# Local attention on TensorE: mask and both halves of a tile's scores issued in one go

## The chip, the cores and the metric

The kernel runs on one core of one Trainium2 chip. The metric is the device time of that core in microseconds (us); less is better. Of the engines the text uses the profile's short names: PE is TensorE (matrix products and transposes), DVE is VectorE, ACT is ScalarE, POOL is GpSimd, SP issues DMAs.

## What is computed

The reference has two residual layers; the part that takes most of the time, and the only one that the change touches, is a stack of six local-attention layers on 8 sequences of 512 tokens with 128 features, 16 heads of 64, windows of 32:

```python
for i in range(DEPTH):            # DEPTH = 6
    x = attn_layer(shift_tokens(x), Wqkv[i], q_scale[i], k_scale[i], Wo[i]) + x
    x = ffn_layer(shift_tokens(x), ln_g[i], ln_b[i], W1[i], b1[i], W2[i], b2[i]) + x

# attn_layer, per head: q and k normalised and rotated; each window of 32 queries sees
# its own 32 keys and the 32 before them
mask = (it < jb) | (it > jb + w) | (jb == -1)
sim = jnp.einsum('bhwie,bhwje->bhwij', bq, bk2) * QK_SCALE
sim = jnp.where(mask, -jnp.finfo(sim.dtype).max, sim)
attn = jax.nn.softmax(sim, -1)
out = jnp.einsum('bhwij,bhwje->bhwie', attn, bv2)

# ffn_layer
a, gate = jnp.split(hg, 2, -1)
return a * jax.nn.gelu(gate, approximate=False) @ W2 + b2
```

All of it is in float32, the mask excepted, which is added as a bf16 product.

## The kernel before

The kernel has three passes. The first (up to about 1190 us) does the global attention, the experts and the chunked attention; the last one adds and writes out. Between them stands `transformer`, the local-attention pass. It runs a hardware loop over the six layers, and in each trip of it the eight sequences are written out, so there are 48 passes through one list of steps, which the text calls trips. A trip mixes two sequences: it begins the attention of one while the rest of the one before (tile 3's scores and outputs, the feed-forward part) still has to be done.

The order of the steps within a trip is the list `BODY`, written by hand (L190 to L199), and every engine walks through it, doing its own share of each step. A sequence is four tiles of 128 tokens, and the first number of a step is its tile `t`: `qk.t.j` and `v.t.j` are projections (one product, 128 rows by 512 columns), `t.t.j` turns a quarter of the queries (j = 0, 1) or keys (2, 3), `sa.t` and `s.t.p` are the scores of a tile for the two parities p of heads, `n` and `w` are work of DVE and ACT alone (norms; sums of the softmax), `pt.t.k` turns half of the probabilities, `oa.t` and `o.t.p` multiply them by the values, `y` is the output projection, `xt`, `xn`, `gate.c`, `up.c` and `y2` are the feed-forward part. Nothing on PE leaves this order: the engine works through it one instruction after the other, and waits where a semaphore isn't there yet.

The list of a trip is:

```python
BODY = [step(name) for name in """
    qk.0.0 t.3.0 qk.0.1 t.3.1 t.3.2 qk.0.2 t.3.3 qk.0.3 n.0 pt.2.0 qk.1.0 sa.3
    v.0.0 pt.2.1 s.3.0 s.3.1 v.0.1 t.0.0 t.0.1 w.3 t.0.2 qk.1.1 t.0.3 oa.2
    qk.1.2 o.2.0 o.2.1 qk.1.3 pt.3.0 sa.0 n.1 pt.3.1 v.1.0 s.0.0 s.0.1 qk.2.0
    v.1.1 t.1.0 w.0 t.1.1 oa.3 t.1.2 qk.2.1 o.3.0 o.3.1 t.1.3 qk.2.2 pt.0.0
    qk.2.3 v.2.0 sa.1 pt.0.1 qk.3.0 s.1.0 s.1.1 n.2 w.1 y v.2.1 t.2.0
    t.2.1 xt oa.0 t.2.2 t.2.3 o.0.0 o.0.1 qk.3.1 pt.1.0 pt.1.1 xn qk.3.2
    qk.3.3 sa.2 v.3.0 gate.0 s.2.0 s.2.1 gate.1 up.0 gate.2 v.3.1 w.2 oa.1
    up.1 up.2 n.3 o.1.0 o.1.1 y2
""".split()]
```

What PE does for a tile's scores is in `fill` (L1445). At `sa.t` it takes the two banks of PSUM (waiting for their last readers) and waits for the copies of the turned queries and keys, writes the mask into both (8 products in bf16, L1458) and does the first half of the products, `score_half` with pairs 0 to 3 (L1424). At `s.t.0` it does the second half (pairs 4 to 7); at `s.t.1` it does nothing. A product there uses 64 rows of the array and makes 32 by 64 results; 32 products make a half, which show as 64 records, since a float32 product is carried out twice. Two such steps per tile, four tiles per trip.

The eight banks of PSUM go round in a ring: the step that fills a bank waits until the reader of the step eight slots before is through. `sa` and `oa` have no slot of their own; they take those of `s` and `o`.

After a tile's scores DVE takes the row maxima and subtracts them (`negmaxl`, `probl`), ACT takes the exponential, DVE sums, POOL multiplies by the reciprocals (L1394), and PE turns the result (`pt`, L1502). After a projection of queries or keys DVE multiplies by the rotation tables (`cs`, L1691), ACT squares, DVE sums, ACT makes the reciprocal norms (L1558, L1559), and POOL adds the rotated halves (L1368) and multiplies by the norms (`qk`, L1377), four operations per tile; PE then turns the result (`t`, L1497). In the feed-forward part ACT computes the gelu (`gel`, L1605), DVE the gated product (`hf`, L1722), and PE the last product `y2` (L1528), which DVE adds to the state; the next trip's first rotations stand behind that on DVE.

The tail after the 48 trips (`OF_LAST`, L200) does what the last sequence has left; in it `sa.3` stands directly before `s.3.0`.

Of the kernel before, what the change touches and what calls it, by code (L numbers as in the profile page):

```python
# [40 lines left out]
PAIRSL = INNER // P  # L41
# [48 lines left out]
def settle(eng, passed):  # L90

    eng.sem_inc(passed, 1)  # L92
# [65 lines left out]
PARITIES = 2  # L158
# [1015 lines left out]
def transformer(nc, io, sh, buf, ctx, order):  # L1174

    last_part = order is OF_LAST
    ident, identb, maskw, state, psum = sh.ident, sh.identb, sh.maskw, sh.state, sh.psum
# [9 lines left out]
    def sem(name):  # L1187
        return ctx.enter_context(nc.semaphore(name + ("_tail" if last_part else "")))
# [46 lines left out]
    def readers(key):  # L1235
        kind, at = key[0], key[1:]
        if kind == "qk":
            return [(squared, at)]
        if kind == "v":
            return [(vcopied, at)]  # L1240
        if kind == "t":
            return [(tcopied, at)]
        if kind == "s":
            return [(centered, at)]
        if kind == "pt":
            return [(turned, at)]
        if kind == "o":
            return [(ocopied, at)]
        if kind == "y":
            return [(mid, "xm")]  # L1250
        if kind == "xt":
            return [(ffn, "x2")]
        if kind == "xn":
            return [(affine, "x2T")]
        if kind == "gate":
            return [(gelued, at[0])]
        if kind == "up":
            return [(hidden, at[0])]
        return [(left, "state")]

    ring = Ring(sem("filledl"), [(key, readers(key)) for key in order if key[0] not in ("n", "w", "sa", "oa")])

    def wait_made(steps, eng, it, key, before):

        (steps.wait_before if before else steps.wait)(eng, it, key)
# [12 lines left out]
    with nc.Block() as block:  # L1278
# [135 lines left out]
        def _(pe):  # L1414
# [3 lines left out]
            def score_half(t, banks, pairs):  # L1418
                last = [None, None]
                for c in pairs:  # L1420
                    for w in range(4):
                        for p in range(PARITIES):
                            rows = slice(64 * p, 64 * p + 64)
                            last[p] = nc.tensor.matmul(  # L1424
                                banks[p][WIN * w:WIN * w + WIN, c * WK:(c + 1) * WK],
                                qTl[rows, t % 2, c, WIN * w:WIN * w + WIN],
                                kTl[rows, c, t * P + WIN * w:t * P + WIN * w + WK],
                                start=False, stop=True, skip_group_check=True)
                return last
# [15 lines left out]
            def fill(it, l, s, key):  # L1445
                kind, at = key[0], key[1:]
                if kind in ("n", "w") or kind in ("s", "o") and at[1] == 1:
                    return
                t = at[0] if at else 0
                if kind == "sa":  # L1450
                    turned_k = (tcopied, tcopied.n + tcopied.at[t, 3])
                    banks = [psum[b] for b in ring.take_both(pe, it, [("s", t, p) for p in range(PARITIES)], [turned_k])]
                    settle(pe, passed)
                    for w in range(4):
                        own = slice(WIN * w, WIN * w + WIN)
                        for p in range(PARITIES):
                            rows = slice(64 * p, 64 * p + 64)
                            nc.tensor.matmul(banks[p][own, :].rearrange("p (c k) -> p c k", k=WK), tiled[rows, own],  # L1458
                                             maskw[rows, min(t, 1), :].unsqueeze(1).to_broadcast([64, PAIRSL, WK]),
                                             start=True, stop=False, skip_group_check=True)  # L1460
                    score_half(t, banks, range(PAIRSL // 2))
                    return
                if kind == "s":
                    last = score_half(t, [psum[ring.bank(("s", t, p))] for p in range(PARITIES)], range(PAIRSL // 2, PAIRSL))
                    for p in range(PARITIES):
                        ring.steps.done(last[p], ("s", t, p))
                    return
                if kind == "oa":
                    turned.wait(pe, it, (t, 0))
                    wait_made(vcopied, pe, it, (t, 1), t >= 2)  # L1470
                    pe.wait_ge(vmoved[t], (l * B + s + (1 if t >= 2 else 2)) * (16 * MOVES[t]))
                    settle(pe, passed)
                    banks = [psum[b] for b in ring.take_both(pe, it, [("o", t, p) for p in range(PARITIES)])]
                    settle(pe, passed)
                    output_half(t, banks, range(2))
                    return
                if kind == "o":
                    turned.wait(pe, it, (t, 1))
                    settle(pe, passed)
                    last = output_half(t, [psum[ring.bank(("o", t, p))] for p in range(PARITIES)], range(2, 4))  # L1480
                    for p in range(PARITIES):
                        ring.steps.done(last[p], ("o", t, p))
                    return
                if key == ("qk", 0, 0):
                    fetched.wait_before(pe, it, "xw")
                ps = psum[ring.take(pe, it, key)]
                if kind in ("qk", "v"):
                    if t == 0:
                        settle(pe, passed)
                        pe.wait_ge(qkv_loaded[at[1] + (4 if kind == "v" else 0)], l * 16 + 16)  # L1490
                    col = (4 if kind == "v" else 0) * BANK + at[1] * BANK
                    last = nc.tensor.matmul(ps[:, :], xw[:, t * P:(t + 1) * P], wqkv[:, col:col + BANK],  # L1492
                                            start=True, stop=True)
                elif kind == "t":
                    wait_made(rotated, pe, it, at, t == T - 1)
                    for c in range(4):
                        last = nc.tensor.transpose(ps[:, c * P:(c + 1) * P], qk[:, at[1], c * P:(c + 1) * P], ident[:, :])  # L1497
                elif kind == "pt":
                    k = at[1]
                    wait_made(weighed, pe, it, at, t == 2)  # L1500
                    for c in range(4):
                        last = nc.tensor.transpose(  # L1502
                            ps[:, c * P:(c + 1) * P],
                            probl[:, t % 2, 4 * k + c, :, :].rearrange("p two k -> p (two k)"), ident[:, :])
                elif kind == "y":
                    pe.wait_ge(o_loaded, rest_loads(l, s) * 16)
                    ocopied.wait(pe, it, (T - 1, 1))
                    for c in range(PAIRSL):
                        last = nc.tensor.matmul(ps[:, :], wol[:, c, :], oTl[:, c, :],  # L1509
                                                start=(c == 0), stop=(c == PAIRSL - 1))  # L1510
                elif kind == "xt":
                    pe.wait_ge(ffn_loaded, rest_loads(l, s) * (16 * FFN_LOADS))
                    mid.wait(pe, it, "xm")
                    for c in range(T):
                        last = nc.tensor.transpose(ps[:, c * P:(c + 1) * P], xm[:, c * P:(c + 1) * P], ident[:, :])
                elif kind == "xn":
                    ffn.wait(pe, it, "x2")
                    for c in range(T):
                        last = nc.tensor.transpose(ps[:, c * P:(c + 1) * P], x2[:, c, :], ident[:, :])
                elif kind in ("gate", "up"):  # L1520
                    if key == ("gate", 0):
                        affine.wait(pe, it, "x2T")
                    col = (DI if kind == "gate" else 0) + sum(CW[:t])
                    last = nc.tensor.matmul(ps[0:CW[t], :], w1l[:, col:col + CW[t]], x2T[:, :], start=True, stop=True)  # L1524
                else:
                    hidden.wait(pe, it, 2)
                    for c, m in enumerate(CW):
                        last = nc.tensor.matmul(ps[:, :], w2l[0:m, c, :], hf[0:m, c, :], start=(c == 0), stop=(c == 2))  # L1528
                ring.steps.done(last, key)
# [371 lines left out]
```

## Time and profile before

| | us |
|---|---|
| median of 3 runs | 4568.3 (4567.04 to 4571.56) |
| span of the profiled execution | 4564.8 |
| first pass | about 0 to 1190 |
| local attention, 48 trips of some 67.2 | 1212.5 to 4401 |
| tail and last pass | 4401 to 4564.8 |
| PE busy | 4319.8 (95%) |
| DVE, ACT, POOL busy | 3279.7 (72%), 2761.6 (60%), 2196.0 (48%) |

The profile is one execution. Times in its rows count from the start of the span. A row of a timeline is a run of instructions of one line and one shape; in brackets stands the idle time of the engine before it and what released it ("issue": nothing that the profile shows). On PE consecutive instructions overlap, so that rows that follow each other without idle time may start before the one before has ended.

### The profile page before, as it was taken

Reading aid. Unit: us, or ns where it says so; the run is one execution under the profiler, and the core shown is the slowest. Engines: PE = TensorE matmul, PEld = TensorE weight load, DVE = VectorE, ACT = ScalarE, POOL = GpSimd, SP = SyncE. Lnnn points to the kernel's source line nnn. Section 1 sums busy time; section 2 is a strip of 40 time slices with the busy share of each in tenths; the row PEclk is TensorE's granted clock in tenths of the full one; section 3 lists DMA queues with packets and bytes.
Section 4 is the critical chain, followed back from the end, with each engine's and each line's share of the span. In section 5 each row is a group of like instructions: output and inputs, shape, how many; then the busy total and the mean of one; then the engine's idle time right before and its main releaser. Section 6 shows DMA issues by size and latency. Waiting matters only on the chain. (4 is left out here: it accounts for less than half of the span.)

```text
span 4564.8 us, 172744 instructions
## 1 busy us (share of the span) xinstructions
PE 4319.8 (95%) x68794; PEld 2569.1 (56%) x68794; DVE 3279.7 (72%) x5779; ACT 2761.6 (60%) x5481; POOL 2196.0 (48%) x1997
## 2 busy tenths in 40 slices
PE   7999999998699999999999999999999999999995
PEld 4555555555455555655555655655555555556553
DVE  4666666665577777877787777777777777777772
ACT  4544555554466666666666666666666666666663
POOL 0000000000466766766666666666666666676661
PEclk9999999999899999999999999999999999999996
DMA  1000000000121112211121112211121111221112
GB/s 39 8 8 6 8 8 4 8 6 3 48 53 49 48 49 63 52 49 50 42 72 50 47 47 61 58 48 44 49 63 52 49 49 46 65 53 49 48 44 65
DMA packets 145061, 189.72 MB, mean 42 GB/s; under 512 B 34151, under 2 KB 66298, under 8 KB 144250
## 3 DMA queue, kind: packets, MB, share of 16 engines
q1 hardware_dynamic: 144250, 178.39, 14.4%
q8 instruction: 572, 9.37, 0.8%
q14 instruction: 239, 1.96, 0.1%
HBM read 29.39 MB, written 4.19 MB: 7 GB/s over the span
## 5 line engine op out<-in xcount | busy, mean ns | idle before, releaser
L1368 POOL TENSOR_TENSOR cs<-cs 128x512 f32<-128x512 f32 x768 | 978.1, 1277 | 527.5 <-DVE cs L1691 523.4
L1492 PE MATMUL psum<-wqkv,xw 128*128 128x512 f32 x2304 | 1191.8, 609 | 34.6 <-DVE tiled L1632 26.3
L1691 DVE TENSOR_TENSOR cs<-psum,rots 128x1024 f32<-128x1024 f32 x768 | 933.9, 1221 | 230.1 <-PE psum L1492 223.5
L1377 POOL TENSOR_TENSOR qk<-cs,rn 128x512 f32<-128x512 f32 x768 | 777.2, 1044 | 330.2 <-ACT rn L1559 305.9
L1575 ACT ACTIVATE sq<-psum 128x512 f32<-128x512 f32 x768 | 459.0, 598 | 611.9 <-DVE cs L1691 577.2
L1403 POOL MEMSET qTl<- 128x2048 f32 x1 | 1.8, 1805 | 1171.2 <-POOLq L516 1171.2
L1645 DVE TENSOR_REDUCE ss<-sq 128x8 f32<-128x512 f32 x768 | 520.0, 677 | 7.0
L1439 PEld LDWEIGHTS psum<-pT,vw 64*64 64x64 f32 x18624 | 401.2, 135 | 182.3 <-issue 181.8
L1497 PEld LDWEIGHTS psum<-ident,qk 128*128 128x128 f32 x3088 | 356.9, 142 | 226.4 <-issue 164.2
L1492 PEld LDWEIGHTS psum<-wqkv,xw 128*128 128x128 f32 x2304 | 368.7, 190 | 199.0 <-issue 172.9
L1497 PE MATMUL psum<-ident,qk 128*128 128x128 f32 x3088 | 444.9, 278 | 21.4 <-POOL qk L1377 16.1
L1439 PE MATMUL psum<-pT,vw 64*64 64x32 f32 x18624 | 446.3, 221 | 3.9 <-issue 2.6
L1394 POOL TENSOR_TENSOR probl<-probl,rs 128x512 f32<-128x512 f32 x386 | 394.9, 1045 | 52.0 <-DVE rs L1678 51.5
L1439 PE MATMUL psum<-pT,vl 64*64 64x32 f32 x6208 | 394.3, 220 | 4.3 <-issue 4.3
L1424 PEld LDWEIGHTS psum<-kTl,qTl 64*32 64x32 f32 x24704 | 302.1, 105 | 146.7 <-issue 135.1
L1424 PE MATMUL psum<-kTl,qTl 64*32 64x64 f32 x24704 | 342.8, 223 | 12.5 <-issue 12.3
L1509 PE MATMUL psum<-oTl,wol 128*128 128x512 f32 x784 | 351.3, 601 | 1.3 <-ACT oTl L1593 1.3
L1696 DVE TENSOR_REDUCE negmaxl<-psum 128x8 f32<-128x512 f32 x386 | 248.2, 685 | 129.2 <-PE psum L1424 129.2
L1565 ACT ACTIVATE probl<-probl 128x512 f32<-128x512 f32 x386 | 233.9, 629 | 164.7 <-DVE probl L1658 163.9
L1439 PEld LDWEIGHTS psum<-pT,vl 64*64 64x64 f32 x6208 | 327.2, 135 | 8.2 <-issue 7.3
L1577 ACT COPY vl<-psum 128x512 f32<-128x512 f32 x384 | 223.0, 581 | 178.2 <-PE psum L1492 177.6
L1524 PE MATMUL psum<-x2T,w1l 128*114 128x512 f32 (+1 forms) x588 | 287.3, 612 | 1.8 <-ACT x2T L1581 1.1
(207 smaller groups left out, 6762.3 us busy)
## 6 DMA issues: line engine op xcount, KB each, us to landing
vw<-vl SPq DMA_DIRECT2D x768, 128.0 KB, 2.4
vw<-vl SPq DMA_DIRECT2D x672, 64.0 KB, 2.0
wqkv<-in_wqkv SPq DMA_DIRECT2D x42, 256.0 KB, 3.7
wol<-in_wol SPq DMA_DIRECT2D x7, 512.0 KB, 4.0
w1l<-in_w1l SPq DMA_DIRECT2D x7, 341.0 KB
xin<-in_x SPq DMA_DIRECT2D x9, 256.0 KB, 2.8
xr<-in_x SPq DMA_DIRECT2D x8, 256.0 KB, 3.0
sums<-sumout SPq DMA_DIRECT2D x8, 256.0 KB, 2.3
```

Of the source, the lines that this page charges most:

```text
L1368: summed_rot.done(nc.gpsimd.tensor_tensor(own, own, halves(cs[:, t % 2, j, 1, :])[:, :, ::-1, :], ALU.add), at)
L1377: rotated.done(nc.gpsimd.tensor_tensor(qk[:, j, :].rearrange("p (h c) -> p h c", c=EL), cs[:, t % 2, j, 0, :].rearrange("p (h c) -> p h c" ...
L1394: weighed.done(nc.gpsimd.tensor_tensor(p, p, r.unsqueeze(2).to_broadcast([P, 8, WK]), ALU.mult), (t, k))
L1424: last[p] = nc.tensor.matmul(banks[p][WIN * w:WIN * w + WIN, c * WK:(c + 1) * WK], qTl[rows, t % 2, c, WIN * w:WIN * w + WIN], kTl[rows, c ...
L1439: last[p] = nc.tensor.matmul(banks[p][64 * half:64 * half + 64, k * P + WIN * w:k * P + WIN * w + WIN], values(t, w, p)[:, c * EL:(c + 1) ...
L1492: last = nc.tensor.matmul(ps[:, :], xw[:, t * P:(t + 1) * P], wqkv[:, col:col + BANK], start=True, stop=True)
L1497: last = nc.tensor.transpose(ps[:, c * P:(c + 1) * P], qk[:, at[1], c * P:(c + 1) * P], ident[:, :])
L1509: last = nc.tensor.matmul(ps[:, :], wol[:, c, :], oTl[:, c, :], start=(c == 0), stop=(c == PAIRSL - 1))
L1524: last = nc.tensor.matmul(ps[0:CW[t], :], w1l[:, col:col + CW[t]], x2T[:, :], start=True, stop=True)
L1575: squared.done(nc.scalar.activation(sq[:, n % 2, :], ps[:, :], ACT.Square), at)
L1645: summed.done(V.tensor_reduce(ss[:, piece[0] % 2, 8 * j:8 * j + 8], sq[:, j % 2, :].rearrange("p (h c) -> p h c", c=EL), AX.X, ALU.add), p ...
L1691: parts.done(V.tensor_tensor(cs[:, t % 2, j, :, :].rearrange("p i (h c) -> p i h c", c=EL), twice, by_head, ALU.mult), at)
```

## The change

At `sa.t` PE now does nothing. What it did there (taking the banks, the wait for the turned keys, the mask) is done at `s.t.0`, and the products of all eight pairs follow it in one call. `BODY` isn't changed, nor is the work of any other engine or the number of instructions.

```diff
@@ -1448,6 +1448,8 @@
                     return
                 t = at[0] if at else 0
                 if kind == "sa":
+                    return
+                if kind == "s":
                     turned_k = (tcopied, tcopied.n + tcopied.at[t, 3])
                     banks = [psum[b] for b in ring.take_both(pe, it, [("s", t, p) for p in range(PARITIES)], [turned_k])]
                     settle(pe, passed)
@@ -1458,10 +1460,7 @@
                             nc.tensor.matmul(banks[p][own, :].rearrange("p (c k) -> p c k", k=WK), tiled[rows, own],
                                              maskw[rows, min(t, 1), :].unsqueeze(1).to_broadcast([64, PAIRSL, WK]),
                                              start=True, stop=False, skip_group_check=True)
-                    score_half(t, banks, range(PAIRSL // 2))
-                    return
-                if kind == "s":
-                    last = score_half(t, [psum[ring.bank(("s", t, p))] for p in range(PARITIES)], range(PAIRSL // 2, PAIRSL))
+                    last = score_half(t, banks, range(PAIRSL))
                     for p in range(PARITIES):
                         ring.steps.done(last[p], ("s", t, p))
                     return
```

Four places of a trip change on PE: tile 3's mask and first half move behind `v.0.0` and `pt.2.1`, tile 0's behind `pt.3.1` and `v.1.0`, tile 1's behind `pt.0.1` and `qk.3.0`, tile 2's behind `v.3.0` and `gate.0`. The two lines that are gone shift the lines below them by one, so L1492 becomes L1491, L1497 becomes L1496 and L1502 becomes L1501; the mask moves from L1458 to L1460, and the scores stay at L1424.

PE before, at tile 3's scores. L1492 is a projection, L1502 turns probabilities, L1458 is the mask, L1424 the scores, L1497 turns queries; REGISTER_ALU rows belong to waits.

```order
L1492 MATMUL psum<-wqkv,xw 128x512
L134 REGISTER_ALU x2
L1458 MATMUL psum<-maskw,tiled 32x512 x8
L1424 MATMUL psum<-kTl,qTl 32x64 x32
L77 REGISTER_ALU
L1492 MATMUL psum<-wqkv,xw 128x512
L1502 MATMUL psum<-ident,probl 128x128 x4
L1424 MATMUL psum<-kTl,qTl 32x64 x32
L77 REGISTER_ALU
L1492 MATMUL psum<-wqkv,xw 128x512
L1497 MATMUL psum<-ident,qk 128x128 x4
```

And the same place after.

```order
L1491 MATMUL psum<-wqkv,xw 128x512
L77 REGISTER_ALU
L1491 MATMUL psum<-wqkv,xw 128x512
L1501 MATMUL psum<-ident,probl 128x128 x4
L134 REGISTER_ALU x2
L1460 MATMUL psum<-maskw,tiled 32x512 x8
L1424 MATMUL psum<-kTl,qTl 32x64 x64
L77 REGISTER_ALU
L1491 MATMUL psum<-wqkv,xw 128x512
L1496 MATMUL psum<-ident,qk 128x128 x4
```

The wait for the banks and the turned keys (L134), the mask and 32 products have moved behind a projection and a transpose step, and the 64 products stand together.

PE before, at tile 1's scores; L1509 is the output projection `y`.

```order
L1502 MATMUL psum<-ident,probl 128x128 x4
L77 REGISTER_ALU
L1492 MATMUL psum<-wqkv,xw 128x512
L77 REGISTER_ALU
L1492 MATMUL psum<-wqkv,xw 128x512
L134 REGISTER_ALU
L1458 MATMUL psum<-maskw,tiled 32x512 x8
L1424 MATMUL psum<-kTl,qTl 32x64 x32
L1502 MATMUL psum<-ident,probl 128x128 x4
L1492 MATMUL psum<-wqkv,xw 128x512
L1424 MATMUL psum<-kTl,qTl 32x64 x32
L1506 ISA
```

And after.

```order
L1501 MATMUL psum<-ident,probl 128x128 x4
L77 REGISTER_ALU
L1491 MATMUL psum<-wqkv,xw 128x512
L77 REGISTER_ALU
L1491 MATMUL psum<-wqkv,xw 128x512
L1501 MATMUL psum<-ident,probl 128x128 x4
L1491 MATMUL psum<-wqkv,xw 128x512
L134 REGISTER_ALU
L1460 MATMUL psum<-maskw,tiled 32x512 x8
L1424 MATMUL psum<-kTl,qTl 32x64 x64
L1505 ISA
L1508 MATMUL psum<-oTl,wol 128x512 x8
```

Here the second transpose step of tile 0's probabilities and the first projection of tile 3 come ahead of the mask.

## Rows read from the trace of the kernel before

**Rows 1.** Busy time by engine (instructions), PEclk, DMA: one trip.
```profile
2983.20:3050.40 67.20, 66.20 (x1245) 40.15 (x1244) 52.98 (x84) 44.47 (x83) 45.13 (x41) 1.00 0.18 48
```

**Rows 2.** Timeline of PE around tile 3's scores: start, length, work [idle before, releaser].
```profile
2983.22 1.02 PE L1492 MATMUL psum<-wqkv,xw 128*128 128x512 f32 x2
2984.76 0.41 PE L1458 MATMUL psum<-maskw,tiled 64*32 64x512 bf16 x8 [0.52 <-ACT kTl L1588]
...
2988.04 1.13 PE L1492 MATMUL psum<-wqkv,xw 128*128 128x512 f32 x2
...
2990.67 0.66 PE L1497 MATMUL psum<-ident,qk 128*128 128x128 f32 x4 [0.28 <-POOL qk L1377]
```

**Rows 3.** Waits of PE: line, what it waited for, us in total, times, longest.
```profile
PE psum L1458 <- ACT kTl L1588: 28.7, 47, 1.7
...
PE psum L1497 <- POOL qk L1377: 16.1, 72, 0.3
PE psum L1424 <- issue: 12.3, 27, 0.8
```

**Rows 4.** Timeline of PE around tile 1's scores, up to the output projection.
```profile
3007.61 1.02 PE L1492 MATMUL psum<-wqkv,xw 128*128 128x512 f32 x2
3008.47 0.60 PE L1502 MATMUL psum<-ident,probl 128*128 128x128 f32 x4
3008.91 1.88 PE L1492 MATMUL psum<-wqkv,xw 128*128 128x512 f32 x4
3010.72 0.41 PE L1458 MATMUL psum<-maskw,tiled 64*32 64x512 bf16 x8
3010.95 0.84 PE L1424 MATMUL psum<-kTl,qTl 64*32 64x64 f32 x64
3011.72 0.66 PE L1502 MATMUL psum<-ident,probl 128*128 128x128 f32 x4
3012.21 1.02 PE L1492 MATMUL psum<-wqkv,xw 128*128 128x512 f32 x2
...
3014.06 7.11 PE L1509 MATMUL psum<-oTl,wol 128*128 128x512 f32 x16
```

**Rows 5.** Timeline of PE in the tail, where both halves stand together.
```profile
4478.99 1.46 PE L1424 MATMUL psum<-kTl,qTl 64*32 64x64 f32 x128
4480.40 0.32 PE L1439 MATMUL psum<-pT,vw 64*64 64x32 f32 x8
```

**Rows 6.** Timeline of POOL, the norms of tile 0.
```profile
2987.56 4.05 POOL L1377 TENSOR_TENSOR qk<-cs,rn 128x512 f32<-128x512 f32 x4 [1.06 <-ACT rn L1559]
```

**Rows 7.** Timeline of PE, the turning of tile 1's queries, two steps.
```profile
3002.35 1.04 PE L1497 MATMUL psum<-ident,qk 128*128 128x128 f32 x8
```

**Rows 8.** Timeline of POOL: the norms of tile 1, tile 0's probabilities weighed.
```profile
3000.54 4.05 POOL L1377 TENSOR_TENSOR qk<-cs,rn 128x512 f32<-128x512 f32 x4 [1.05 <-ACT rn L1559]
...
3005.85 2.05 POOL L1394 TENSOR_TENSOR probl<-probl,rs 128x512 f32<-128x512 f32 x2
```

**Rows 9.** Timeline of PE around tile 2's scores and at the trip's last product.
```profile
3028.69 1.88 PE L1492 MATMUL psum<-wqkv,xw 128*128 128x512 f32 x4
...
3034.34 1.97 PE L1524 MATMUL psum<-x2T,w1l 128*114 128x512 f32 x4
...
3041.99 2.84 PE L1528 MATMUL psum<-hf,w2l 114*128 114x512 f32 x6
```

**Rows 10.** Timeline of DVE: tile 3's third rotation and the last hidden products.
```profile
3029.75 1.23 DVE L1691 TENSOR_TENSOR cs<-psum,rots 128x1024 f32<-128x1024 f32 x1 [0.35 <-PE psum L1492]
...
3040.31 1.56 DVE L1722 SCALAR_TENSOR_TENSOR hf<-psum,b1l,gel 114x512 f32<-114x512 f32 x2 [0.96 <-ACT gel L1605]
```

**Rows 11.** Timeline of ACT, the first of three table loads.
```profile
3033.83 1.28 ACT L1605 ACT_TABLE_LOAD   x1
```

**Rows 12.** Timeline of PE: the second half of tile 0's scores in a later trip.
```profile
3201.62 0.76 PE L1424 MATMUL psum<-kTl,qTl 64*32 64x64 f32 x53
3203.14 0.33 PE L1424 MATMUL psum<-kTl,qTl 64*32 64x64 f32 x11 [0.77 <-issue]
```

## The prediction

> **What bounds the kernel now.** I read the windows view first: of one trip of the local-attention pass, 67.2 us, TensorE (PE) is busy 66.2; the next engine is busy 53.0 [rows 1]. So the pass, 48 such trips, goes at PE's pace, and a microsecond that PE saves is kept unless somebody else sets a later point of the trip. Such points are found in three views: PE's own timeline (an idle time with a releaser behind it), the list of waits, and the timelines of the producers (does their row follow straight on the row before). The granted clock of the trip is 1.00, the higher of the two levels (2.4 GHz) [rows 1], so the durations need no correction.
>
> What the timeline shows best is not how long a row lasts but when the next one starts; records overlap, and the difference of starts is what a step costs. All prices below are such differences.
>
> **Prices.** From the second tile's neighbourhood [rows 4]: a projection step costs 0.86 us (3007.61 to 3008.47), a transpose step 0.44 (3008.47 to 3008.91), two projections of which the second stands before a mask 1.81 (3008.91 to 3010.72), so the one before the mask 0.95. The mask costs 0.23, the first half of the scores 0.77, the transpose step behind it 0.49, that is 0.05 more than the same step elsewhere. The pattern: each passage between 128-row and 64-row work costs PE 0.09 going in and 0.05 (transposes) coming out. In the tail, where no step stands between the halves, 128 score records go in 1.41 us (4478.99 to 4480.40) [rows 5], where two halves cost 2 x 0.77 = 1.54. So not ending and restarting the block is worth 0.13.
>
> **Part 1, around tile 1 (kept).** Before, from 3008.91 to the start of the output projection at 3014.06: 5.15 us [rows 4]. After, the same steps in the new order: two projections 1.72, the transpose step 0.44, the projection before the mask 0.95, mask 0.23, scores 1.41; that is 4.75 by these prices, a saving of 0.40 in this trip; adding up the price differences alone (0.13 + 0.09 + 0.05) gives 0.27, the rest is a slow end of the second half here. I take 0.33, between the two. The steps that now go first, 1 us earlier, find what they need: the transposes, from about 3010.6, need the probabilities that POOL weighed from 3005.85 to 3007.90 [rows 8]. What they fill is read in an order that hasn't changed. Nothing gates PE from here to the output projection, which needs the attention outputs of tile 3, copied before. So 48 x 0.33 = 15.9 us off.
>
> **Part 2, around tile 3 (absorbed).** Largest on paper: from 2983.22 to 2988.04, 4.82 us, of which 0.52 is a wait for the copy of the turned keys [rows 2]; that wait comes 47 times and totals 28.7 us [rows 3]. After: 0.86 + 0.86 + 0.53 (a transpose step before a mask: 0.44 + 0.09) + 0.23 + 1.41 = 3.89, the mask over 0.7 us later, so the wait goes: 0.93 us less. But soon after, the transposes at 2990.67 wait 0.28 for POOL's normalised queries [rows 2], and POOL's row there is four operations in a train from 2987.56 [rows 6], started by ACT's reciprocal norm and so by projections that stand ahead of the moved steps. This wait (72 times, 16.1 us [rows 3]) only grows by what PE saves. Value: 0. If the train were not there it would be 45 us.
>
> **Part 3, around tile 0 (mostly absorbed).** By the same prices 0.30. Then follows the turning of tile 1's queries, a step at 3002.35 and one 0.44 later [rows 7]; the second needs the second operation of POOL's train from 3000.54, a fourth of 4.05 us each, so 3002.56 [rows 8]; it starts at 3002.79, and a step that really waits starts 0.07 after its producer (2990.67 after 2987.56 + 3 x 1.01). Slack 0.16 in this trip. The same subtraction over the eight sequences of a layer gives about nothing for the first two, 0 to 0.26 for the next two, and over 0.2 for the last four, which carry a pause (part 5). I book 1.6 us for the first four in all, and weigh the others' 0.2 to 0.3 against the longer pause there, net 1 us.
>
> **Part 4, around tile 2 (nearly absorbed).** 3028.69 to 3034.34 is 5.65 [rows 9]; after: 3 x 0.86 + 0.95 + 0.23 + 1.41 = 5.17, less by 0.48. But the trip's last product, at 3041.99, follows DVE's hidden product, which ends at 3040.31 + 1.56 = 3041.87 and waited 0.96 for ACT's gelu [rows 9, 10]. ACT works without a gap from the table load at 3033.83 on [rows 11], through three loads of 1.28, and is brought there by DVE's product at 3029.75, which waited for a projection ahead of the mask [rows 10]. So the train starts before the moved place. The product starts 0.12 after its producer where 0.07 is the least: 0.05 x 48 = 2.4 us off.
>
> **Part 5, fetching instructions (a cost).** At 3201.62 the second half of a score block stops after 53 records and goes on 0.77 us later with nothing released ("issue") [rows 12]; such pauses inside scores come 27 times, 12.3 us in all, 0.46 on the mean [rows 3]. They fall in blocks where PE takes very many short instructions in little time. The old order gave two projections or transposes, few and long, between two stretches of 64 records; the new one takes 8 + 128 records in 1.64 us. A point that was reached late enough can now be reached too early. Where it happens depends on the position in the program, which repeats for all six layers. My estimate: around tiles 0, 1 and 3 as much as now or absorbed; around tile 2 a further two to four of the eight sequences of a layer pause beyond what the train of part 4 hides, at 0.46 three times a layer, 3 x 0.46 x 6 = 8 us. Both ends: nothing (0), and one pause of 0.77 in every second block of the three places not fully absorbed, 48 x 3 / 2 x 0.77 = 55, less some 20 that the trains hide: 35.
>
> The Trainium skill ("Runtime: NRT & Kernel Launch", Instruction fetch mechanics) says an engine's instructions are streamed in blocks of 256 and that passing a block's end is mostly hidden. By that rule this term would be 0 and the time 4548; the 0.77 us row speaks against it.
>
> **Sum.** -15.9 - 1.6 - 1 - 2.4 + 8 = -12.9 us; I take -12, since starts of other blocks drift a little. Against the profiled execution's 4564.8 that is 4553; the median of the runs stands 3.5 above it, so **4556**. The rest, the two other passes and the tail (there the first step stood next to the second already), is unchanged; no instruction is added or removed, and no other engine's order moves.
>
> **Rivals.**
> *No new pauses.* Parts 1, 3, 4 alone, and part 3 kept in the four late sequences too (24 x 0.3 = 7): -16 - 1.6 - 7 - 2.4 = -27 at most, -20 with part 3's slacks as read; 4541 to 4548. For: only 27 pauses now. Against: they lie in second halves, right where the dense stretch ends.
> *Every change of mode is paid on the path.* If the trains of parts 3 and 4 started with PE and moved with it, everything but tile 3 would be kept: 48 x (0.30 + 0.33 + 0.48) = 53, so 4515. Against: the rows above, where the train's head stands ahead of the moved place. The Trainium skill ("TensorEngine Tiling (Array Packing)", Key Properties) says that changing the tiling mode drains TensorE; by it halving the changes pays everywhere, and the trace agrees on the price (0.86 against 0.95) but not on the path.
> *Nothing to tell.* Pauses of about 20 us eat the savings of tile 1: 4564 to 4571.
> *Slower: the dense block outruns the fetch.* Mechanism of part 5, at the blocks of tiles 1 and 2 (nobody hides it at tile 1). It decides from 16 + 5 = 21 us, that is 46 more pauses of 0.46, or about one in four of the 192 blocks; at the upper end 35 - 20 = +15, so 4583.
>
> **How the numbers follow.** Forecast case (4549 to 4563) 0.42; no new pauses 0.20; everything kept 0.06; nothing to tell 0.15; slower 0.17. A measurement of this kernel can tell about 0.2%, 9 us, from no change, so faster means below 4559: two thirds of the forecast case (0.28) and the two cases below, 0.54. Slower means above 4577: 0.13 of the 0.17. Same takes the rest, 0.33. The range for 8 in 10 goes from 4538 (leaves out "everything kept" and a little) to 4581.
>
> **What the changed profile would show.** Right: 128 score records in one row, next start 1.41 later; the wait for turned keys gone from the list and the wait for POOL's queries up from 16 to some 50 us; the wait for the hidden product in over 30 trips; from tile 1's region 0.33 less. Pauses inside scores, now 12.3 us, at 15 to 30. Wrong: pauses above 35 us (slower), or a wait for weighed probabilities or for a bank before the moved steps, or the transposes of tile 1 never waiting (more gain than forecast).

## The result and the profile after

The changed kernel takes 4597.1 us (median of 4 runs, 4594.77 to 4600.97); the kernel before, run beside it, 4569.5 (4567.04 to 4571.56). The ratio is 1.0063, with a 95% interval from 1.0049 to 1.0078: slower by 27.6 us, where 4556 was forecast and 4581 was the upper end.

The profiled execution has a span of 4593.8 us. The windows view of the local-attention pass, before and then after (stretch: its length, then busy time and instructions of PE, weight loads, DVE, ACT, POOL; granted clock; DMA share; GB/s):

```profile
1212.50:4401.00 3188.50, 3114.31 (x58375) 1882.72 (x58376) 2492.61 (x3922) 2087.61 (x3855) 2117.05 (x1925) 1.00 0.19 52
```

```profile
1207.60:4430.00 3222.40, 3076.78 (x58374) 1879.92 (x58375) 2490.00 (x3923) 2088.89 (x3855) 2118.09 (x1924) 1.00 0.19 51
```

PE is busy 37.5 us less, as it should be with half the passages into and out of the tiled work, and yet from the first trip's start to the last one's it is 34 us longer (both views begin with the first trip, which in this execution starts 4.7 us earlier after the change, so that the span grows by 29.0 only). So PE stands idle some 70 us more, at the same granted clock. The list of waits of the changed kernel says at what (it answers to [rows 3]):

```profile
PE psum L1424 <- issue: 60.5, 50, 2.5
PE psum L1496 <- POOL qk L1377: 52.1, 131, 0.6
...
PE psum L1523 <- issue: 10.2, 6, 2.0
PE psum L1439 <- issue: 9.1, 19, 1.3
PE psum L1527 <- DVE hf L1721: 5.7, 25, 0.9
```

The 28.7 us of waits for the turned keys are gone. The wait for POOL's queries has grown from 16.1 to 52.1 us and takes their place; neither moves the end. What moves it is the first row: pauses inside the scores for which the profile knows no releaser, 60.5 us where there were 12.3, and another 10.2 in the gate projections behind them (L1523), where there were 0.8.

Where they lie is seen when the starts of all steps are laid side by side over the 48 trips (the sums here and below are worked out from the timelines, after less before):

| stretch of a trip | sum over the pass, us |
|---|---|
| around tile 3's scores, and up to the waits for POOL that follow | -44.4 + 46.7 |
| around tile 0's scores and the next stretch | -3.0 + 2.1 |
| around tile 1's scores, up to the output projection | -8.2 |
| around tile 2's scores | +30.1 |
| the gate and up projections and tile 1's outputs behind them | +10.8 |
| the rest | +1.4 |
| all 48 trips | +35.6 |

Tile 2's place is the loss, and not in all sequences: the first three of each layer gain 0.49 us per trip there, the last five lose 1.1 to 1.6. Two trips of one layer show both. The timeline of PE in the third sequence (start, length, work):

```profile
3044.11 2.74 PE L1491 MATMUL psum<-wqkv,xw 128*128 128x512 f32 x6
3046.69 1.04 PE L1523 MATMUL psum<-x2T,w1l 128*114 128x512 f32 x2
3047.66 0.41 PE L1460 MATMUL psum<-maskw,tiled 64*32 64x512 bf16 x8
3047.89 1.46 PE L1424 MATMUL psum<-kTl,qTl 64*32 64x64 f32 x128
3049.28 2.83 PE L1523 MATMUL psum<-x2T,w1l 128*114 128x512 f32 x6
```

and in the eighth:

```profile
3392.07 1.04 PE L1523 MATMUL psum<-x2T,w1l 128*114 128x512 f32 x2
3393.04 0.41 PE L1460 MATMUL psum<-maskw,tiled 64*32 64x512 bf16 x8
3393.27 1.06 PE L1424 MATMUL psum<-kTl,qTl 64*32 64x64 f32 x86
3395.39 0.67 PE L1424 MATMUL psum<-kTl,qTl 64*32 64x64 f32 x42 [1.06 <-issue]
3395.99 2.40 PE L1523 MATMUL psum<-x2T,w1l 128*114 128x512 f32 x5
```

From 3044.11 to 3049.28 it is 5.17 us, to the hundredth what the prediction's prices gave against 5.65 before [rows 9]. In the eighth sequence 128 records take 2.72 us in place of 1.39, because PE stops after record 86. In all six layers the stop comes after the same record.

### The profile page after: what moved, and what is told of

It reads as the page before. It is cut to its first block and busy times, and to the rows that moved or that the text cites. A ratio compares the mean times of both kernels' runs of the same rounds, so it can differ in the third digit from the quotient of the medians.

```text
span 4593.8 us, 172744 instructions
## 1 busy us (share of the span) xinstructions
PE 4276.0 (93%) x68794; PEld 2564.1 (56%) x68794; DVE 3277.2 (71%) x5779; ACT 2762.9 (60%) x5481; POOL 2197.3 (48%) x1997
## 3 DMA queue, kind: packets, MB, share of 16 engines
q8 instruction: 572, 9.37, 0.9%
## 5 line engine op out<-in xcount | busy, mean ns | idle before, releaser
L1491 PE MATMUL psum<-wqkv,xw 128*128 128x512 f32 x2304 | 1167.6, 605 | 37.3 <-DVE tiled L1631 26.3
L1491 PEld LDWEIGHTS psum<-wqkv,xw 128*128 128x128 f32 x2304 | 377.1, 190 | 238.4 <-issue 221.6
L1496 PEld LDWEIGHTS psum<-ident,qk 128*128 128x128 f32 x3088 | 355.2, 142 | 275.6 <-issue 163.0
L1496 PE MATMUL psum<-ident,qk 128*128 128x128 f32 x3088 | 449.6, 279 | 56.4 <-POOL qk L1377 52.1
L1424 PE MATMUL psum<-kTl,qTl 64*32 64x64 f32 x24704 | 306.4, 224 | 60.8 <-issue 60.5
L1424 PEld LDWEIGHTS psum<-kTl,qTl 64*32 64x32 f32 x24704 | 291.3, 105 | 82.9 <-issue 69.7
L1523 PE MATMUL psum<-x2T,w1l 128*114 128x512 f32 (+1 forms) x588 | 294.5, 625 | 11.3 <-issue 10.2
```

What stands on the lines that cost most here:

```text
L1424: last[p] = nc.tensor.matmul(banks[p][WIN * w:WIN * w + WIN, c * WK:(c + 1) * WK], qTl[rows, t % 2, c, WIN * w:WIN * w + WIN], kTl[rows, c ...
```

## The experiments

The theory, F: PE's instructions come in blocks of 16 KB (the instruction queue has 572 packets and 9.37 MB in both kernels, so 16.4 KB each), a block's end falls at a fixed record of the program, and if it falls late in a dense stretch, the next block isn't there. Rivals: D, that a merged block costs something wherever it stands; G, that the late place is the cause, by what stands ahead of it.

### One place at a time

In both kernels only one tile's scores are treated as in the change, and all others as in the kernel before (for tile 2 it is `t == 2`). The edit against the changed kernel, with cuts marked by three dots; what is left out issues the second half at `s.t.0` where `late` is false:

```diff
-                if kind == "sa":
+                late = t == 1
...
+                if kind == "sa" and late:
                     return
-                if kind == "s":
+                if kind == "sa" or (kind == "s" and late):
...
+                    if not late and not early:
+                        score_half(t, banks, range(PAIRSL // 2))
+                        return
                     last = score_half(t, banks, range(PAIRSL))
...
```

`early` is empty in all these runs.

> Only tile 1's mask and scores are merged at the later place; tiles 0, 2 and 3 as before. Theory F (the loss is pauses of instruction supply in merged blocks, most of it at tile 2): the savings at tile 1 stay, some 8 us as the trace of the changed kernel has them between the third projection of tile 2 and the output projection, so 4557 to 4563, with pauses in scores near the 12 us of before plus 4 to 6. Rival D (a merged block costs the same wherever it stands): a quarter of the 28 us lost, +7, so 4572 to 4578.

Measured: 4558.1 us beside 4565.8, ratio 0.9981 (0.9972 to 0.9991).

> Only tile 2's mask and scores are merged at the later place. Theory F: this place alone carries the loss; in the changed kernel's trace the stretches from tile 3's third projection to the third gate projection and on to the last product are 41 us longer in sum, and two or three of that are hidden later; so 4600 to 4612 against 4568 to 4570, pauses in scores some 40 us above before, in the sequences 4 to 8 of each layer and none in the first three. Rival D: +7, 4575.

Measured: 4607.3 us, ratio 1.0094 (1.0077 to 1.0111), and pauses inside scores of 47.0 us. Tile 1's place gains 8, tile 2's alone loses 41. D, by which both had to lose 7, is out.

### Moving the whole loop against the blocks

The next three add nothing inside the layer loop. They put semaphore increments on PE ahead of it (128 here, 256 in the third), where PE waits for DVE anyway, so that every instruction of the loop stands further on in the program:

```diff
             ring.steps.prime(pe)
+            if not last_part:
+                for _ in range(128):
+                    settle(pe, passed)
             pe.wait_ge(made, MADE)
```

> The changed kernel with 128 semaphore increments on PE ahead of the layer loop, in a time in which PE waits 26 us for DVE anyway; nothing inside the loop changes, but every instruction of it stands half a 16 KB block further on. Theory F: the pauses move. Where blocks end, counted from the pauses seen so far: in tile 2's merged block record 92 of 128 in the first sequence and 81 to 21 in the others (before the shift 124, 114, 104, 95, 85 in sequences 4 to 8), so tile 2 pauses in one sequence in place of five; tile 3's block pauses in four sequences (125, 114, 104, 94) in place of one, partly hidden. Sum: -40 there, +10 to +12 at tile 3, so 20 to 30 us faster than the unshifted changed kernel: 4567 to 4577. Theory G (the pauses come from what stands ahead of the merged block, the wait for the feed-forward input above all): no change, 4595 to 4599.

Measured: 4552.6 us beside 4565.8, ratio 0.9977 (0.9965 to 0.9990). The changed kernel, order and work untouched, is some 40 us faster than without the shift (0.9977 against 1.0063), and now 13 us faster than the kernel before. Expected was 4567 to 4577; the direction and the place were right, the gain was larger, because pauses at tile 3's place are hidden wholly (1.0 to 1.7 us each, in sequences 4 to 7; PE would have waited for POOL) and those at tile 0's shrank as well. Pauses inside scores are still 33.5 us in all, but 18.6 of them stand at tile 3's place. The same trip of the same layer as above, eighth sequence (the added lines move all line numbers by three):

```profile
3362.26 1.04 PE L1526 MATMUL psum<-x2T,w1l 128*114 128x512 f32 x2
3363.23 0.41 PE L1463 MATMUL psum<-maskw,tiled 64*32 64x512 bf16 x8
3363.45 1.46 PE L1427 MATMUL psum<-kTl,qTl 64*32 64x64 f32 x128
3364.84 2.83 PE L1526 MATMUL psum<-x2T,w1l 128*114 128x512 f32 x6
```

No pause. G, by which nothing had to change, is out as it stood.

> The kernel before with the same 128 increments ahead of the loop. Theory F: its 12 us of pauses in scores and 7 in outputs move too, by position; tile 0's second halves, where most were, are then ended by records 39 to 8 in the first four sequences and should be free; -6 to +3 us. Theory G: nothing.

Measured: 4566.7 us, ratio 1.0001 (0.9992 to 1.0011), pauses in scores 13.9 us. The shift by itself is worth nothing to the old order, whose pauses in scores stay near the 12.3 us they had.

> The changed kernel with 256 increments, twice the shift of the first test. If the blocks are 256 instructions, everything comes back to where it stood without a shift: 4592 to 4602, and pauses in tile 2's scores in sequences 4 to 8. If what mattered with 128 was the delay or the increments themselves, it stays at 4550.

Measured: 4616.5 us (2 runs), ratio 1.0115 (1.0097 to 1.0134): the pauses are back, so that neither the delay nor the increments themselves made the gain with 128, and the time is 14 us above the upper end of what was expected. Both are in the list of waits:

```profile
PE psum L1427 <- issue: 57.3, 50, 2.5
PE psum L1494 <- issue: 55.1, 13, 44.0
```

The first row is the changed kernel's 60.5 again, and the stretches of the loop sum to +34.9 against the kernel before, where the unshifted changed kernel had +35.6. The second row holds a wait of 44.0 at the start of the pass, where it was 26.3: 256 increments take longer than the wait that was to hide them (44.0 / 256 = 0.17 us each), and the pass starts some 18 us later. So the period is 256 instructions, and the increments are free only up to about 150 of them (26.3 / 0.17, an estimate).

The traces show the period directly. If all records of PE's instruction stream (matrix products, weight loads and waits) are counted from the first score record of a layer, a layer has 20658 of them, and the place of each pause over 0.15 us with releaser "issue" can be taken modulo 256. In the changed kernel 82 of 87 such pauses in the six layers, in scores, projections and outputs alike, start at place 182 to 184; with 128 increments 60 of 65 at 54 or 55, which is 128 less; with 256, 80 of 86 at 182 to 184 again. In the kernel before 43 of 49 start at 197 to 199, the same places of the program, since the first score record stands 15 instructions earlier there. Five of the others in each stand where the loop returns to its start.

The two alignments together give each merged block at 16 different positions. The record at which the 16 KB block ends (counted on from the pauses seen, good to some three records) and the time of the 128 records, mean of six layers:

| ends at record | tile 3 | tile 0 | tile 1 | tile 2 |
|---|---|---|---|---|
| 7 to 30 | 1.39 | 1.43 to 1.70 | 1.44 to 1.52 | 1.39 |
| 31 to 61 | 1.39 | 1.63 to 1.70 | 1.48 to 1.60 | 1.39 to 1.51 |
| 71, 72 | 1.39 | 1.58 | 1.61 | 1.43 |
| 81, 82 | 1.39 | 1.84 | 1.55 | 1.48 |
| 85 | 1.39 | | | 3.01 |
| 92 to 96 | 1.91 (3.47 at a layer's start) | 1.85, 1.95 | 1.74 | 2.97, 3.02 |
| 102 to 115 | 2.13, 2.29 | 2.13 to 2.35 | 1.66 to 1.83 | 3.30, 3.48 |
| 124, 125 | 2.91 | 2.18 | 1.75 | 3.17 |

Position rules: up to record 82 there is little (tile 0 has pauses in three of its six layers there), from about 85 to 95 on there is a pause. How long it is depends on the tile, 0.3 at tile 1 and 1.6 to 2.1 at tile 2. That difference needed a second look.

### What makes the pause at tile 2 so long

Theory F1 supposes that the next block of instructions is called for at a point within the block before, and that the call is held up if PE's instruction stream stands at a wait ahead of that point. At tile 2 the change put such a wait ahead: the first gate projection waits for the normalised input `x2T` (L1580 on ACT), which in the eighth sequence is made from 3391.08 to 3391.89, just before the projection starts at 3392.07. Before the change the bank waits, the mask and 64 records stood in front of that wait. Theory F2: the pause follows from the density alone.

The first test moves seven eighths of tile 2's records to the early place.

```diff
-                    score_half(t, banks, range(PAIRSL // 2))
+                    score_half(t, banks, range(PAIRSL - 1 if t == 2 else PAIRSL // 2))
...
```

The part left out starts the second step at `PAIRSL - 1` for tile 2.

> Tile 2 alone: seven eighths of the products (112 records) with the mask at the first place, ahead of the third value projection and the first gate projection with its wait; the last 16 records at the second place. All else as before, no shift. Theory F1 (a pause comes where a block of instructions ends late in a dense stretch, and is 1.5 us longer if the wait of the gate projection stands ahead of the stretch, because the instructions that call for the next block are held behind it): pauses in sequences 5 to 7 of a layer only (the block ends at record 110, 100 and 89 of the early part), each 0.5 to 1.2 us instead of 1.6 to 2.1, partly hidden: 4570 to 4582. Theory F2 (density alone): sequences 5 to 8, 1.6 to 2.1 us each, as with the late place: 4595 to 4607. Theory G (the late place alone, whatever the blocks): 4562 to 4568.

Measured: 4601.4 us, ratio 1.0082 (1.0066 to 1.0097). By the time alone that is F2's. The timelines say otherwise: it was sequences 6 and 7 that paused, and 8 did not. In sequence 6, then in 8:

```profile
3251.66 1.57 PE L1424 MATMUL psum<-kTl,qTl 64*32 64x64 f32 x111
3254.94 0.21 PE L1424 MATMUL psum<-kTl,qTl 64*32 64x64 f32 x1 [1.72 <-issue]
```

```profile
3394.30 0.41 PE L1458 MATMUL psum<-maskw,tiled 64*32 64x512 bf16 x8
3394.53 1.40 PE L1424 MATMUL psum<-kTl,qTl 64*32 64x64 f32 x112
```

Sequence 8 has the block's end at record 89 here and goes through in 1.32 us in this layer, where with the late place record 85 was enough for 3.01. The expectation was out by some ten records (PE stops after record 111 in sequence 6 and 101 in sequence 7; the early part has fewer instructions ahead of it), so that sequence 5 was free, its block ending behind the 112. And the pauses that were left were not short, 1.3 to 1.9 us, and nothing hid them: the 12 trips are 26 us longer at this place. F1 was right that sequence 8 is free and wrong on how long the others pause. It says more than that: here the gate projection's wait stands behind the dense stretch, and the pauses are nearly as long as with the late place. So it isn't that wait alone that makes them long.

The second test leaves the dense block where the change has it and moves only the waits for the banks and the mask back to the early place:

```diff
-                    score_half(t, banks, range(PAIRSL // 2))
+                    if t != 2:
+                        score_half(t, banks, range(PAIRSL // 2))
...
-                    last = score_half(t, [psum[ring.bank(("s", t, p))] for p in range(PARITIES)], range(PAIRSL // 2, PAIRSL))
+                    last = score_half(t, [psum[ring.bank(("s", t, p))] for p in range(PARITIES)], range(0 if t == 2 else PAIRSL // 2, PAIRSL))
```

> Tile 2 alone, no shift: the waits for the banks and the mask stay at the first place, all 128 score records are at the second. The dense block is the one of the late place within 16 instructions; what changes is that the instructions between the waits and the mask's end stand ahead of the gate projection's wait again. Theory F1 (the next block of instructions is called for about 64 instructions into the one before, and not while PE's sequencer stands at a wait ahead of that point): in sequences 7 and 8 the call now goes out 2 to 4 us earlier and their pauses go, in 5 and 6 they stay: 4584 to 4598. Theory F2 (only the record at which the block ends counts): all stay, 4603 to 4611.

Measured: 4578.4 us beside 4567.0, ratio 1.0028 (1.0018 to 1.0038), against 1.0094 with mask and scores together at the late place. PE's timeline in the eighth sequence of the same layer:

```profile
3377.53 0.41 PE L1458 MATMUL psum<-maskw,tiled 64*32 64x512 bf16 x8
3377.87 1.13 PE L1493 MATMUL psum<-wqkv,xw 128*128 128x512 f32 x2
3378.83 1.02 PE L1525 MATMUL psum<-x2T,w1l 128*114 128x512 f32 x2
3379.78 1.48 PE L1424 MATMUL psum<-kTl,qTl 64*32 64x64 f32 x128
3381.20 2.83 PE L1525 MATMUL psum<-x2T,w1l 128*114 128x512 f32 x6
```

The same 128 records, in the same place, without the pause: 1.41 us in every layer in sequence 8, and in five of six layers in sequence 7. Sequences 4 to 6 still pause, by about 1.0 us instead of 1.8 to 2.1. On 7 and 8 F1 was right and F2 is out. But F1 had the pauses of 5 and 6 stay as they were, and the time is 6 us below the lower end of its range, because they were halved. When the block of instructions arrives can be read from the DMA view, asked for two neighbouring stretches. The changed kernel, from 3386.5 to 3392.8 has no packet of the instruction queue; from 3392.8 to 3395.0:

```profile
q8 instruction: 1, 0.02, 2.8%
```

that is after the gate projection's wait, and PE goes on at 3395.39. With the mask early, from 3372.0 to 3377.5, ahead of the gate projection:

```profile
q8 instruction: 1, 0.02, 1.5%
```

and none from 3377.5 to 3381.2, the whole dense block. Counted from the step `xn`, which stands before either place, the packet starts 4.0 us later in the changed kernel. What was lost is lead.

What takes the lead can be read closer than F1 has it. The records of PE's sequencer in the traces have the last wait ahead of the dense block, and the instruction queue's packets have their starts. Both are counted here from the block's first score record, in us, minus for earlier; the last column is what the block takes beyond 1.39, on the mean:

| place, sequences | last wait | packet starts | beyond 1.39 |
|---|---|---|---|
| changed kernel, tile 1, 1 and 2 | -2.7 | -1.4 to -0.5 | 0.4 |
| changed kernel, tile 0, 5 to 7 | -2.1 to -1.8 | -0.9 to -0.2 | 0.8 |
| mask early, tile 2, 4 to 6 | -1.6 | -0.6 to 0.1 | 1.0 |
| changed kernel, tile 2, 4 to 6 | -0.9 to -0.8 | 0.3 to 1.1 | 1.9 |
| seven eighths early, tile 2, 6 and 7 | -0.8 | 0.2 to 1.0 | pauses of 1.3 to 1.9 |

In all rows but the third the last wait is that for the banks; there it is the gate projection's. The nearer to the dense block PE's stream was last held, the later the packet and the longer the pause, whichever wait it is. That would also explain why tile 1 loses 0.4 and tile 2 1.9 at about the same records. It fits all five rows; no run moves the bank waits alone, without the 16 instructions of the mask, so which of the two counts stays open.

### A version that merges only where it is safe

> No shift. Merged are the blocks which a 16 KB block's end meets at record 82 or before (tile 0 in sequences 1 to 4, tile 1 in 4 to 8, tile 2 in 1 to 3, tile 3 in 2 to 8 of each layer); the 13 others of 32 are split as before. Theory F: all that was lost comes from the 13, so this is faster than the kernel before: by the stretches of the changed kernel's trace tile 1 gives 6, tile 2 4 and tile 0 1 us, so 4553 to 4560. Rival D (each merged block costs): 19 of 32 of the loss, 4582 to 4590.

```diff
...
+                late = s in {0: (0, 1, 2, 3), 1: (3, 4, 5, 6, 7), 2: (0, 1, 2), 3: (1, 2, 3, 4, 5, 6, 7)}[t]
...
```

`s` is the sequence counted from 0; the rest of the edit is that of one place at a time.

Measured: 4554.4 us beside 4567.0, ratio 0.9975 (0.9965 to 0.9984), pauses in scores 8.0 us, fewer than the kernel before has. With 19 of the 32 blocks of a layer merged and none of them at a bad record it is as fast as was forecast for all 32; the 13 others make the difference of some 40 us to the changed kernel (0.9975 against 1.0063).

> The changed kernel with 160 increments ahead of the loop. Theory F, from the two shifts known: tile 2's block is ended at record 76 or before in all sequences, below the 85 from which it paused, so no pause of more than 0.2 us there (with 128: one sequence of eight, 7 us in all); the outputs of tile 0 are ended at records 49 to 18 in place of 55 to 34, worth 2 to 4 us; tile 1 the same. So 6 to 12 us faster than with 128: 4540 to 4548.

Measured: 4549.8 us beside 4565.5, ratio 0.9966 (0.9954 to 0.9978). Pauses in scores are 17.3 us. The 160 increments reach 3 us past the wait that hides them, and outputs of tile 0 and 1 are now met badly (21.3 us of pauses at the outputs, 14.2 with 128); it is 2 to 10 us short of what was expected.

> The kernel before with 160 increments. It tells what of the gain of the shift is the change's and what the shift alone gives. Theory F: its pauses in scores move from the second halves in which they were; by the table of record against pause 0 to 8 us faster than with 128, so 4558 to 4567, and the changed kernel at the same shift 12 to 22 us faster than this one.

Measured: 4567.6 us, ratio 1.0003 (0.9994 to 1.0012), 0.6 above the range expected. At the same shift the change is worth 18 us.

> 152 increments (some 26 us, as long as PE waits there for DVE; 160 took 3 us more than that) and everything merged but tile 0 in the first sequence, whose block would be met at record 91. By the table of records no pause over 0.2 us at tile 2, and the 3 us at the start are saved: 4543 to 4550.

Measured: 4550.7 us beside 4567.0, ratio 0.9966 (0.9955 to 0.9977). The same as with 160, and 0.7 us above the upper end of what was expected. The wait at the start is 28.1 us where it was 29.4 with 160 increments, so only 1.3 of the 3 us came back, and the pauses are not fewer (23.0 us in scores, 23.3 in outputs, in the profiled execution).

The best versions, with 152 or 160 increments, are 16 us faster than the kernel before and by the ratios some 44 us faster than the changed one as it stands. They hold only for this very program: whatever is added ahead of the loop moves the blocks' ends.

## Why the prediction was wrong

**Prices and new order: right.** 5.17 us for tile 2's stretch was forecast and measured; 128 records in a row cost 1.39 where 1.41 was taken from the tail.

**Part 2, tile 3, absorbed: right.** PE is 0.95 us earlier after the scores and waits as much longer for POOL, in every undisturbed trip; the list's 52.1 us stand against the "some 50" of the forecast. Even pauses of up to 1.7 us vanish in it (with 128 increments).

**Part 4, tile 2, nearly absorbed: right for the saving.** In the first three sequences 0.49 was saved and 0.26 of it given back before the last product, so 0.23 was kept, more than the 0.05 forecast; the last product waits for DVE in 25 trips, where over 30 were forecast.

**Part 1, tile 1: right in sign, half in size.** 8.2 us in place of 15.9 (7.6 in the run with tile 1 alone). Of the difference, the blocks there take 1.5 to 1.6 us where 1.43 is the least, and the first three sequences pause, 0.3 us each.

**Part 3, tile 0:** -0.9 us with what follows, 2.6 forecast.

**Part 5, instruction supply: the step that failed.** The mechanism was named, and as the rival "slower: the dense block outruns the fetch" it had its row, its price and a chance of 0.17; the term was put at +8 and its bound at +35. Measured are 60.5 + 10.2 us of pauses against 12.3 + 0.8, and tile 2's place with what follows it is 41 us longer, its own savings already taken off. Two things were wrong in the sizing. First, the price: I took 0.46 us, the mean of the pauses before, as the price of a new one. Those were pauses in stretches of 64 records with sparse steps in front of them. At tile 2 a stretch of 136 whose block ends late takes 1.6 to 2.1 us more than 1.39. Second, the place: I counted only density, and overlooked the waits. The bank waits and the mask, moved behind `gate.0`, stand right before the 128 records, and the packet with the next block starts 0.3 to 1.1 us after the first of them in sequences 4 to 6, where with the mask put back it starts up to 0.6 us before. The prediction listed what each moved step needs; it should have asked too where the instruction stream is last held before the dense block. The test with the mask put back shows what this was worth: its 48 trips sum to +13.3 us, those with all of tile 2 at the late place to +38.7, so some 25 us.

And where the blocks end could have been had from the trace of before: the records at which it paused (x53, then x11 [rows 12]) fix it for every sequence of the layer, 256 instructions apart, and the order then tells at which record of each merged block the end falls: beyond 85 in 5 of 8 sequences at tile 2, not "two to four". That 85 is about where the pauses begin, only the runs after the change tell. The Trainium skill ("Runtime: NRT & Kernel Launch", Instruction fetch mechanics) states the 256, and the run with 256 increments agrees (+34.9 against +35.6 us); its word that passing a block's end is mostly hidden fits the old order (12.3 us of pauses in scores) and not the new one (60.5 us).

## What to carry to other kernels

A long straight program on PE is fed in blocks of instructions, and here a stretch of some hundred short products in a row outran the supply where a block ended in its last third. Before making such a stretch longer, find from the pauses with releaser "issue" where the blocks end, and count on; idle instructions ahead of a loop (128 to 160 here), under a wait that is there anyway, can move all the ends at once. And look at where the engine's stream is last held before such a stretch: here the instructions came the later, the nearer that wait stood.

## What the runs showed of the hardware

- The pauses of PE repeat with a shift of 256 instructions and move with one of 128 (sums over the 48 trips +34.9, +35.6 unshifted, and -14.1 us), and within a kernel they start at one place modulo 256 (82 of 87 in the changed one).
- A packet of the instruction queue lies 0.9 to 1.5 us in its transfer (nine in ten of those in the changed kernel's pass), and after a pause PE goes on 1.2 to 2.0 us after its end, 1.4 on the median. When the packet starts depends on where PE's stream was last held (the table above). Where in a block the call for the next one stands isn't shown: in sequence 8 with the mask early the packet starts 4.5 us before the dense block, earlier than both the last bank wait (2.8) and the gate projection's (1.6).
- A semaphore increment by itself costs PE 0.17 us (44.0 us for 256).
- Without a pause 128 score records take 1.39 us at tiles 2 and 3 and mostly 1.5 to 1.7 at tiles 0 and 1, with hitches of 0.05 to 0.15 us inside. They don't follow the block's end, and their cause wasn't looked for; it stays open.
